# Value product of the second attention reordered: probabilities times context, then the value weights, for two batches at once

## The reference, cut to what matters

```python
qh = (q_in @ wq + bq).reshape(b, q_len, H, K)          # 8 batches x 112 queries, H = 16, K = 128
kh = (kv_in @ wk + bk).reshape(b, t, H, K)             # 375 keys, context width 512
vh = (kv_in @ wv + bv).reshape(b, t, H, K)
kh = concatenate([kh, bias_k]); vh = concatenate([vh, bias_v])   # a 376th key
weights = softmax(einsum('bqhk,bthk->bhqt', qh, kh) / sqrt(K))
ctx = einsum('bhqt,bthk->bqhk', weights, vh).reshape(b, q_len, H * K)
return ctx @ wo + bo
```

## Time and profile before

| what | value |
|---|---|
| median of three runs | 2494.27 us (2492.91 to 2495.61) |
| the profiled execution's own time | 2492.27 us |
| its span in the trace | 2490.4 us |
| PE busy | 2389.4 us, 96% |
| DVE, ACT, POOL busy | 43%, 43%, 23% |
| DMA | 179 MB, 72 GB/s mean |
| mean granted clock of TensorE | 0.985 of full |

### The profile page before, as it was taken

The page is one execution under the profiler, slowest core; times in us unless marked ns, Lnnn a source line. Parts: engine busy times, 40 slices in busy tenths (PEclk is TensorE's granted clock), DMA queues, the critical chain, the costliest instruction groups (busy, mean ns, idle before and its releaser), DMA issues.

```text
span 2490.4 us, 46188 instructions
## 1 busy us (share of the span) xinstructions
PE 2389.4 (96%) x14242; PEld 2135.8 (86%) x14242; DVE 1076.7 (43%) x2377; ACT 1078.0 (43%) x2583; POOL 580.9 (23%) x975
## 2 busy tenths in 40 slices
PE   6999889999999999999999899999999999999899
PEld 5777679988998998998997798998998989988798
DVE  6777663441333333333334523333333333334643
ACT  3777732243444444444443434444444444443321
POOL 4111023240222222223121230223122222212321
PEclk9999889999999999999999999999999999999999
DMA  6110011154112112112214262112112122124120
GB/s 194 41 34 20 10 47 54 48 148 121 40 59 94 53 46 93 59 54 82 71 58 132 66 189 72 59 42 92 59 66 67 59 72 80 58 76 136 38 59 30
DMA packets 196126, 179.32 MB, mean 72 GB/s; under 512 B 53758, under 2 KB 184242, under 8 KB 196018
## 3 DMA queue, kind: packets, MB, share of 16 engines
q1 hardware_dynamic: 196018, 177.97, 23.4%
HBM read 144.89 MB, written 33.05 MB: 71 GB/s over the span
## 4 chain that ended last, share of the span: by engine, by line
PE 82%; issue 8%; DVE 3%; ACT 3%; POOL 2%; DMA 1%; SPq 0%; POOLq 0%; ACTq 0%; DVEq 0%
PE ps_v L1094 9%; PE ps_v L1095 9%; PE ps_v L1096 9%; PE ps_k L1094 9%; PE ps_k L1096 8%; PE ps_k L1095 8%; PE ps_o L1244 6%; PE ps_s L1094 3%; PE ps_s L1096 3%; PE ps_s L1095 3%; PE ps_o L1094 3%; PE ps_o L1096 3%; PE ps_o L1095 3%; PE ps_t L1233 3%; PE ps_t L1174 1%
## 5 line engine op out<-in xcount | busy, mean ns | idle before, releaser
L512 POOL TENSOR_TENSOR cs_lo<-ctx_raw,cs_hi 128x376 fp32r<-128x376 f32 x288 | 284.7, 1020 | 739.0 <-DVE cs_hi L873 739.0
L968 DVE SCALAR_TENSOR_TENSOR k_lo<-ps_k,col_b,k_hi 128x375 fp32r<-128x375 f32 x256 | 155.6, 608 | 678.6 <-ACT k_hi L695 678.6
L1094 PE MATMUL ps_v<-w_b_hi,cs_hi 128*128 128x512 f32 (+1 forms) x928 | 389.4, 420 | 9.1 <-POOL w_b_lo L496 7.5
L1094 PE MATMUL ps_k<-cs_hi,w_a_hi 128*128 128x376 f32 x1152 | 390.2, 339 | 5.7 <-DVE k_lo L968 4.1
L1096 PE MATMUL ps_k<-cs_hi,w_a_lo 128*128 128x376 f32 x1152 | 385.3, 334 | 0.0
L1095 PE MATMUL ps_k<-cs_lo,w_a_hi 128*128 128x376 f32 x1152 | 385.0, 334 | 0.0
L1096 PE MATMUL ps_v<-w_b_hi,cs_lo 128*128 128x512 f32 (+1 forms) x928 | 365.3, 394 | 0.0
L1095 PE MATMUL ps_v<-w_b_lo,cs_hi 128*128 128x512 f32 (+1 forms) x928 | 365.2, 394 | 0.0
L695 ACT ACTIVATE k_hi<-ps_k,col_b 128x375 fp32r<-128x375 f32 x256 | 146.7, 573 | 422.3 <-PE ps_k L1096 422.3
L712 ACT ACTIVATE prob<-ps_s,row_columns 112x376 f32<-112x376 f32 x256 | 147.1, 575 | 222.7 <-DVE row_columns L974 222.7
L1094 PEld LDWEIGHTS ps_k<-cs_hi,w_a_hi 128*128 128x128 f32 x1152 | 217.1, 188 | 18.9 <-issue 6.2
(11 more groups left out here) (197 smaller groups left out, 4545.9 us busy)
## 6 DMA issues: line engine op xcount, KB each, us to landing
ctx_raw<-in_ctx_t SPq DMA_DIRECT2D x72, 752.0 KB, 5.1
w_raw_a<-in_blocks_a SPq DMA_DIRECT2D x104, 256.0 KB, 3.3
w_raw_b<-in_blocks_b SPq DMA_DIRECT2D x104, 256.0 KB, 3.4
q_lo<-q_scratch SPq DMA_DIRECT2D x72, 224.0 KB, 2.5
o_scratch<-o SPq DMA_DIRECT2D x64, 224.0 KB, 2.0
q_scratch<-prob SPq DMA_DIRECT2D x36, 224.0 KB, 2.7
q_scratch<-o SPq DMA_DIRECT2D x36, 224.0 KB, 2.7
cs_hi<-o_scratch SPq DMA_DIRECT2D x6, 672.0 KB, 4.3
```

What stands on the lines that cost most here:

```text
L512: pool.tensor_tensor(cs[place.parity][1][:, part], ctx_raw[place.parity][:, part], cs[place.parity][0][:, part], ALU.subtract).then_inc(cs ...
L968: dve.scalar_tensor_tensor(out=k[t % 2][1][:, 0:LK], in0=ps_k[:, 0:LK], scalar=col_b[:, ds(place.column((C_BK0, C_BK1), t), 1)], in1=k[t % ...
L1094: pe.matmul(out, w_h, m_h, start=first, stop=False)
```

## The change

The values are no longer made. Since weights x (context x Wv) = (weights x context) x Wv, the kernel now sums the context with the probabilities of all four heads of a group (`context_sum`: for each of four slices `d` of 128 context columns, three key tiles x 3 matmuls with 448 moving columns, 4 heads x 112 queries) and multiplies the sums with the value weights (`head_output`: for each head four slices x 3 matmuls with 224 moving columns, 2 batches x 112 queries). `value` and `weighted` of this layer are gone. Both operands of the new products need halves: the turned probabilities (`pt`, hi on ACT, lo on DVE) and the sums (`act_t`, `sum_hi` on ACT, `sum_lo` on DVE). The 376th key enters as a separate term: its probability is taken on DVE (`extra_probability`), stored, loaded back spread over all partitions, and turned into a term by ACT (`extra_term`) that DVE adds when it empties a head (`output`).

The context's halves are kept in memory in two layouts. The transposed halves are stored during the first attention (`store_context`) and loaded for each batch of the second layer (`load_halves`, 2 x 752 KB). A layout by key is a new input; it is loaded, split (`by_key_hi` on ACT, four of its six parts in chunk 1 and two in chunk 2; lo on POOL) and stored (4 x 768 KB) in each of the four steps of the first MLP, two batches a step, and loaded for each batch (`load_by_key`, 2 x 768 KB). DVE's `context_hi` and POOL's `context_lo` are gone from the second layer.

In a pair of batches, the sums of the odd batch before come one in each tile of the even batch, those of the even batch two in each of the last two tiles of the odd one; the heads of the pair before come two in each of the first two tiles of the odd batch, all in one bank (`ps_o[0]`), one before `key` and one behind it. An epilogue does the last batch's four sums and the last pair's four heads. The first group's outputs are now loaded and split after that, as the other groups' are. The first group and the first pairs are written out instead of looped. The core of the diff:

```diff
+        ckd = [[sb(f"ckd{i}_{h}", [P, 3 * D], F32R) for h in ("hi", "lo")] for i in range(2)]
+        pt = [[sb(f"pt{i}_{h}", [P, 3, NT * LQ], F32R) for h in ("hi", "lo")] for i in range(2)]
...
+        ps_c = [ps_v, ps_o[1]]
...
+        def chunks(place, t):
+
+            if place.before() is None:
+                return ()
+            if place.parity == 0:
+                return (t,)
+            return {2: (0, 1), 3: (2, 3)}.get(t, ())
+
+        def heads(place, t):
+
+            return (2 * t, 2 * t + 1) if place.parity and not place.head and t < 2 else ()
+
+        def pair_before(place):
+
+            return place.before().before()
...
+            def store_context(place):
+
+                sp.wait_ge(cs_lo, DT * place.batch + DT)
+                sp.sem_inc(sp_waited, 1)
+                for s in range(2):
+                    dst = ctx_scr[ds(place.b, 1), s].rearrange("o p f -> (o p) f")
+                    sp.dma_start(dst, cs[place.parity][s][:, 0:DT * KW].bitcast(F32)).then_inc(ctx_out[place.parity], 16)
+
+            def load_halves(place):
+
+                for s in range(2):
+                    src = ctx_scr[ds(place.b, 1), s].rearrange("o p f -> (o p) f")
+                    sp.dma_start(cs[place.parity][s][:, 0:DT * KW].bitcast(F32), src).then_inc(ct_in[place.parity], 16)
+
+            def load_by_key(place):
+
+                for s in range(2):
+                    src = kd_scr[ds(place.b, 1), s].rearrange("o p f -> (o p) f")
+                    sp.dma_start(ckd[place.parity][s][:].bitcast(F32), src).then_inc(ck_in[place.parity], 16)
...
+                def one_batch(place):
+                    if not place.final:
+                        load_q(place.next())
+                    if place.after(2):
+                        sp.wait_ge(k_mm, place.tile + NT)
                         sp.sem_inc(sp_waited, 1)
+                        load_halves(place.after(2))
+                    if place.swap:
+                        load_block(0, place.block_a + 2)
+                        if not (isinstance(place.group, int) and place.group == 0):
+                            load_block(1, place.block_b + 1)
+                    store_extra(place)
+                    if place.parity:
+                        if not place.head:
+                            store_pair(pair_before(place))
+                        load_extra(place)
+                    if not place.final and not (place.head and place.parity == 0):
+                        sp.wait_ge(c_mm, NT * place.visit)
+                        sp.sem_inc(sp_waited, 1)
+                        load_by_key(place.next())
...
                 load_block(0, na + 2)
                 if not last:
                     load_block(1, nb + 2)
+                if m == 0:
+                    for parity in range(2):
+                        sp.wait_ge(kd_lo, 6 * fg + 3 * parity + 3)
+                        sp.sem_inc(sp_waited, 1)
+                        for s in range(2):
+                            dst = kd_scr[ds(2 * fg + parity, 1), s].rearrange("o p f -> (o p) f")
+                            sp.dma_start(dst, ckd[parity][s][:].bitcast(F32)).then_inc(kd_out[parity], 16)
+                    if not (isinstance(fg, int) and fg == 3):
+                        load_by_key_raw(fg + 1)
...
+                for part in range(6 if m == 0 else 0):
+                    parity, cols = part // 3, slice(part % 3 * D, (part % 3 + 1) * D)
+                    pool.wait_ge(kd_hi, 6 * fg + part + 1)
+                    pool.tensor_tensor(ckd[parity][1][:, cols], ctx_raw[parity][:, cols], ckd[parity][0][:, cols],
+                                       ALU.subtract).then_inc(kd_lo, 1)
...
+                def sum_hi(place, d):
+                    act.wait_ge(c_mm, NT * place.visit + d + 1)
+                    if d == 0 and place.parity == 0 and not place.head:
+                        act.wait_ge(z_mm, NT * place.pairs)
+                    act.activation(act_t[0][:, d, place.parity * HALF:(place.parity + 1) * HALF], ps_c[d % 2][:, 0:HALF],
+                                   ACT.Identity).then_inc(c_hi, 1)
...
+                def by_key_hi(fg, part):
+                    parity, cols = part // 3, slice(part % 3 * D, (part % 3 + 1) * D)
+                    if part % 3 == 0:
+                        act.wait_ge(kd_in[parity], 16 * fg + 16)
+                        wait(act, kd_out[parity], 32 * fg)
+                    act.activation(ckd[parity][0][:, cols], ctx_raw[parity][:, cols], ACT.Identity).then_inc(kd_hi, 1)
...
+                        part = 4 * (c - 1) + f
+                        if m == 0 and 0 <= part < 6:
+                            by_key_hi(fg, part)
...
+                def turned_lo(place, t):
+                    dve.wait_ge(t_ev, place.unit + t + 1)
+                    dve.tensor_tensor(turned_place(1, place, t), ps_t[t % 2][:, 0:3 * LQ].rearrange("p (i r) -> p i r", i=3),
+                                      turned_place(0, place, t), ALU.subtract).then_inc(t_lo, 1)
+
+                def sum_lo(place, d):
+                    cols = slice(place.parity * HALF, (place.parity + 1) * HALF)
+                    dve.wait_ge(c_hi, NT * place.visit + d + 1)
+                    dve.tensor_tensor(act_t[1][:, d, cols], ps_c[d % 2][:, 0:HALF], act_t[0][:, d, cols],
+                                      ALU.subtract).then_inc(c_lo, 1)
+
+                def output(place, t):
+                    dve.wait_ge(z_mm, NT * place.pairs + t + 1)
+                    dve.wait_ge(z_term, NT * place.pairs + t + 1)
+                    if t == 0 and not place.head:
+                        dve.wait_ge(z_out, 16 * place.pairs)
+                    dve.tensor_tensor(o_pair[:, :, t, :], final_bank(place, t)[:, 0:2 * LQ].rearrange("p (b r) -> p b r", b=2),
+                                      term[t % 2], ALU.add).then_inc(z_ev, 1)
...
+                        for head in heads(place, t)[0:1]:
+                            output(pair_before(place), head)
                         if place.key(t + 3):
                             key_lo(*place.key(t + 3))
+                        for head in heads(place, t)[1:2]:
+                            output(pair_before(place), head)
+                        for d in chunks(place, t):
+                            sum_lo(place.before(), d)
+                        if place.key(t + 1):
+                            turned_lo(*place.key(t + 1))
                         if place.key(t + 2):
                             maximum(*place.key(t + 2))
                             normalized_1(*place.key(t + 2))
...
-                def weighted(place, t):
-                    if t == 0:
-                        pe.wait_ge(v_ev, 3 * place.batch + 3)
-                        pe.wait_ge(xv_in[place.parity], 16 * place.block + 16)
-                    wait(pe, o_ev, NT * place.batch + t - 1)
-                    pe.wait_ge(t_ev, place.unit + t + 1)
-                    for i, n in enumerate(ATT1.vals()):
-                        last = pe.matmul(ps_o[t % 2][:, 0:LQ], v[place.parity][0:n, i, t * P:(t + 1) * P],
-                                         prob_t[t % 2][0:n, i * LQ:(i + 1) * LQ], start=(i == 0), stop=(i == 2))
-                    last.then_inc(av_mm, 1)
+                def context_sum(place, d):
+                    if d == 0:
+                        pe.wait_ge(t_lo, NT * place.visit + NT)
+                        pe.wait_ge(ck_in[place.parity], 32 * place.pairs + 32)
+                    if d >= 2 or not place.head or place.parity:
+                        pe.wait_ge(c_lo, NT * place.visit + d - 1)
+                    for i, (_, n) in enumerate(KEY_TILES):
+                        last = product(ps_c[d % 2][:, 0:HALF],
+                                       [ckd[place.parity][s][0:n, i * D + d * P:i * D + (d + 1) * P] for s in range(2)],
+                                       [pt[place.parity][s][0:n, i, :] for s in range(2)], i == 0, i == 2)
+                    last.then_inc(c_mm, 1)
+
+                def head_output(place, t):
+                    pe.wait_ge(w_lo[1], 4 * place.block_b + t + 1)
+                    if place.final and t % 2:
+                        pe.wait_ge(s_exp, place.unit + NT)
+                    if place.final and t > 1:
+                        pe.wait_ge(z_ev, NT * place.pairs + t - 1)
+                    elif not place.final and (t or not place.head):
+                        pe.wait_ge(z_ev, NT * place.pairs + t)
+                    for c in range(DT):
+                        if t == 0:
+                            pe.wait_ge(c_lo, NT * place.visit + c + 1)
+                        last = product(final_bank(place, t)[:, 0:2 * LQ], [w[1][s][:, c, t * P:(t + 1) * P] for s in range(2)],
+                                       [heads_view(act_t[s][:, c, :], t) for s in range(2)], c == 0, c == DT - 1)
+                    last.then_inc(z_mm, 1)
...
```

(30 more changed lines are left out.)

393 lines of the change are left out of this document (225 added, 168 removed).

## The result

The changed kernel takes 2517.88 us (median of 4 runs, 2516.38 to 2519.88), the kernel before in the same comparison 2493.84 (2492.91 to 2495.61). The ratio is 1.0100, 95% interval 1.0088 to 1.0112. I had forecast 2474. The direction was wrong, the time by 44 us.

The account below looks back on a forecast made before the run. PE bounds the kernel, busy 2389.4 of 2490.4 us. From 2492.3: attention -37, group changes -7, first MLP +24 give 2472, plus 2.0 for the runs' median: 2474 us; own range 2440 to 2510, with rival 1 to 2890.

Parts of the forecast that it names:

- Work lost and gained: Second layer's attention, PE: 11.04 us of matmuls removed and 10.11 added for each batch, net 0.93 us less.
- rival 1: Head matmuls of 224 columns run at the plain fp32 price, 0.387 us each: +422 us, 2874 us; chance 0.33.
- The new wait: Attention: PE waits for DVE to empty the first head before the second; 0.7 us a pair, 0.35 a batch.
- -0.93 a batch: Attention: PE's net change in matmul work for each batch, 11.04 us removed against 10.11 added.
- 37 + 7 = 44: Attention's gains in us: 37 over 64 batches at -0.58, and 7 at group changes, no wait for w_b_lo.
- The first MLP: Raw loads queue behind stores, ACT waits, PE stands 8 us in steps 1, 2 and 3: +24 us.
- 412: First MLP: the time in us near which the raw load was predicted to land.
- Elsewhere ... I take 0: First attention's stores, the gap between attention and projection, and DMA in attention at 160 GB/s: taken as 0 us.
- rival 2: Attention: softmax chain takes 5.2 us instead of 4.5, PE waits 2.7 us a pair: +86, 2560 us; chance 0.10.
- Rival 4: First MLP: its loads run at the low rate, 164 GB/s: 2510 us; chance 0.05.

## Why the prediction was wrong

**Work lost and gained: right.** The sums' pitch is 0.203 against 0.206 taken, the heads' 0.113 against 0.112. The straight line from wider products of the same kind told the price; rival 1, to which I gave 0.33 and the upper end of the range, had no row for it.

**The new wait: mis-sized.** I charged 0.35 us a batch. Most second heads wait under 0.1 us; the list shows 7.6 us for all ten longer waits. The order of my chain is right, DVE does empty the first head behind the normalization (1066.97 to 1067.36), but from the end of the last sum (1063.14) that is 4.2 us and not 4.9, and 4.2 is when PE is there. With -0.93 a batch and nearly no wait, and the waits of the earlier trace rows gone, a group came out 8.1 us shorter, eight of them 65 us, where the sum had 37 + 7 = 44.

**The first MLP: right in its mechanism, too small.** The stall was 8 us three times, from the same cause. The step that failed is "+24 us": it left out the half-speed clock behind each stall, and the stage lost 30.1. I had charged "then the slow clock" to the end of attention in the same text, and not here. That 412 was so near is luck. The DMA rate was 401 GB/s in the stall, above the 311 that I had from the earlier trace rows, and the stores had the queue only from 401.1, when w_b's last column had landed, and not from 399.5; the two errors cancel.

The queue's order, on which this rests, is now shown by the landings: 403.0 to 409.1 for the stores, then 411.0 and 412.8 for the raw loads. The Trainium skill ("DMA: Bandwidth & Descriptors", section "Queues, rings and completion order") says that on each DMA engine the descriptors of one queue are consumed in its order, and the trace agrees with it in these six landings and in the query's store, which landed behind the eight loads issued before it.

**"Elsewhere ... I take 0": this step failed**, and with it the sign. It speaks of the DMA traffic as a rate, "about 3.5 MB a batch, 160 GB/s, half of what the queue has shown", and for the steady part that holds. It doesn't ask what stands behind the large loads in the queue. In the query stage that is a small store, for which ACT waits: 16.9 us of PE's waits, with the slow clock behind, 22 us in the two passes. No term of the sum stood for it, though the prediction had done exactly this walk along SP's queue for the MLP. The same paragraph saw the end of attention and took 0 there; start and end of the two attentions together lost 25 us.

**Not in the sum at all:** the delay of ACT and PE at the jump, 30.2 - 22.3 = 7.9 and 28.0 - 22.3 = 5.7 us, about 14; and the start of attention, 6 us of PE's time in each pass, since the code that filled it was the value product that went.

The ledger by stages:

| part | us |
|---|---|
| eight groups at -8.1 | -65 |
| first MLP | +30 |
| layer norm and queries, two passes | +22 |
| two jumps | +14 |
| start and end of two attentions | +25 |
| the rest | -2 |

They come to +24, the difference of the spans. The 25 us are what is left of attention's -26.3 when the groups and the jumps are taken out, 12.5 a pass. PE stands 6 of them at the start; at the end its waits are 5.9 us where they were 4.4. The other 5 us a pass are not taken apart: some slow clock is in them, and sums and heads that come behind the last scores. Not tried: attention's end by itself.

The forecast's own range was narrower than its ends: heads at 0.106 or 0.120, waits of 0 to 1.5 a pair and 0 to 60 for the MLP add up to 2418 to 2548, not 2440 to 2510. The wider one would have held the measured time, though most of what was missing is in none of its terms.

Of the rivals none happened. Three lay on the slower side. Rival 1's pitch was not there, and rival 2, the waits of the softmax chain, had the wrong place: the list has no wait of PE in the steady tiles. Rival 4's 2510 is the number nearest to 2518, by luck: the MLP's loads ran at 401 GB/s, not at 164.

## What to carry to other kernels

When a change adds large transfers, walk the issuing queue at every place where they enter, and name the small transfer right behind them and who waits for it. Put what is needed soonest first and spread the rest. A mean rate says only that the steady part fits. Charge a stall of PE with the slow clock behind it, here a quarter to a third more. And where an unrolled or rotated loop loses work, look at its start and its jump: what was removed may have been their cover.

## What was not expected of the hardware

- A product of 224 columns in fp32r has a pitch of 0.113 us, half that of 448 (0.203) and a little more: narrowing it costs little.
- At its jump back ACT started 4.9 us after its keys were there with the DMA engines full (3.7 in the second pass), 1.8 with them half busy, and 0.2 with them full and the loop written out.
- A store of 224 KB took 14.2 us to land behind 6.2 MB of loads in its queue; the transfers of a queue landed in the order of their issue.
- The 16 DMA engines moved 401 GB/s over 12 us, above the 311 of the program's start.
